# One row-sum addition of 2048 columns instead of two of 1024 in the self attention of a diffusion block

## The reference, cut to what matters

```python
def _attn(xq, ctx, wq, wkv, wo, bo):
    q = _heads(xq @ wq)
    k, v = jnp.split(ctx @ wkv, 2, axis=-1)
    ...
    q = _rope(q, sq, cq)
    k = _rope(k, sk, ck)
    sim = jnp.einsum('bhnd,bhmd->bhnm', q, k) * DH ** (-0.5)
    a = jax.nn.softmax(sim, axis=-1)
    o = jnp.einsum('bhnm,bhmd->bhnd', a, v)
    o = o.transpose(0, 2, 1, 3).reshape(xq.shape[0], xq.shape[1], MID)
    return o @ wo + bo
attn_in = _adaln(x, cond, ln1_w, ln1_b, g1_w, g1_b, b1_w, b1_b)
x = _attn(attn_in, attn_in, sa_wq, sa_wkv, sa_wo, sa_bo) + x
...
```

## Time and profile before

| | |
|---|---|
| time, median of 3 runs | 2244.72 us (2241.64 to 2246.07) |
| the profiled execution's own time | 2244.09 us |
| its span in the profile | 2242.2 us |
| TensorE (PE) busy | 2056.6 us, 92% |
| VectorE (DVE) busy | 1794.6 us, 80% |
| ScalarE (ACT) busy | 1378.4 us, 61% |
| additions at L1098 | 384 + 64, 452.7 + 75.5 us |

### The profile page before, as it was taken

The page is one execution under the profiler, slowest core; times in us unless marked ns, Lnnn a source line. Parts: engine busy times, 40 slices in busy tenths (PEclk is TensorE's granted clock), DMA queues, the critical chain, the costliest instruction groups (busy, mean ns, idle before and its releaser), DMA issues. The chain is left out here.

```text
span 2242.2 us, 40840 instructions
## 1 busy us (share of the span) xinstructions
PE 2056.6 (92%) x16376; PEld 932.5 (42%) x16376; DVE 1794.6 (80%) x2801; ACT 1378.4 (61%) x1748; POOL 35.0 (2%) x26
## 2 busy tenths in 40 slices
PE   4799999999999999999999999997379999986999
PEld 2233333345333335433333533335233444444676
DVE  5888999986899997799999689965768888844654
ACT  4577777765777766677677476762547666633442
POOL 1000000000000000000000000000400000000000
PEclk8799999999999999999999999998589999987999
DMA  5010101111110100111110111003323343324111
GB/s 189 29 39 30 48 30 58 40 39 42 55 39 30 67 37 23 61 45 39 39 39 30 48 59 38 30 20 97 91 81 116 111 124 125 120 73 130 38 39 38
DMA packets 102116, 136.04 MB, mean 61 GB/s; under 512 B 36694, under 2 KB 75176, under 8 KB 101928
## 3 DMA queue, kind: packets, MB, share of 16 engines
q1 hardware_dynamic: 101927, 133.43, 18.2%
HBM read 67.89 MB, written 13.11 MB: 36 GB/s over the span
## 5 line engine op out<-in xcount | busy, mean ns | idle before, releaser
L943 ACT ACTIVATE sa_probs<-sa_ps_s 128x1024 f32<-128x1024 f32 x512 | 496.3, 1021 | 216.1 <-PE sa_ps_s L734 216.1
L749 PE MATMUL sa_ps_o<-sa_probs,sa_v_pair 128*64 128x512 f32 x2048 | 530.9, 610 | 7.4 <-DVE sa_mx L1085 7.4
L1098 DVE TENSOR_TENSOR sa_acc<-sa_acc,sa_probs 128x1024 f32<-128x1024 f32 x384 | 452.7, 1220 | 16.5 <-ACT sa_probs L943 8.2
L1085 DVE CUSTOM_DVE_ANT_0 sa_rise<-sa_ps_t,sa_rise 128x512 f32<-128x512 f32 x504 | 327.1, 686 | 133.9 <-PE sa_ps_t L711 131.1
L931 ACT ACTIVATE sa_rise<-sa_ps_t 128x1024 f32<-128x1024 f32 x252 | 257.4, 1022 | 156.3 <-PE sa_ps_t L704 156.1
L727 PE MATMUL sa_ps_s<-sa_hi 64*128 64x512 f16 x1024 | 197.0, 377 | 0.9 <-ACT sa_raw L917 0.9
L727 PE MATMUL sa_ps_s<-sa_lo,sa_hi 64*128 64x512 f16 x1024 | 197.0, 377 | 0.0
L727 PE MATMUL sa_ps_s<-sa_hi,sa_lo 64*128 64x512 f16 x1024 | 196.8, 377 | 0.0
L749 PEld LDWEIGHTS sa_ps_o<-sa_probs,sa_v_pair 128*64 128x64 f32 x2048 | 114.7, 135 | 164.6 <-issue 96.4
L704 PE MATMUL sa_ps_t<-sa_kd,sa_hi 64*128 64x512 f16 x504 | 99.8, 390 | 33.2 <-ACT sa_raw L917 19.9
L704 PEld LDWEIGHTS sa_ps_t<-sa_kd,sa_hi 64*128 64x128 f16 x504 | 26.1, 93 | 216.6 <-issue 173.5
(11 more groups left out here) (329 smaller groups left out, 4020.7 us busy)
## 6 DMA issues: line engine op xcount, KB each, us to landing
sa_swp<-sa_raw SPq DMA_DIRECT2D x124, 256.0 KB, 2.4
sa_inv<-sa_scratch SPq DMA_DIRECT2D x128, 128.0 KB, 2.9
ca_swp<-ca_raw SPq DMA_DIRECT2D x64, 256.0 KB, 2.4
ca_inv<-ca_scratch SPq DMA_DIRECT2D x64, 256.0 KB, 3.9
sa_xs<-in_x SPq DMA_DIRECT2D x4, 1024.0 KB, 5.8
sa_xr<-in_x SPq DMA_DIRECT2D x4, 1024.0 KB, 5.8
cap_xs<-x_after_self SPq DMA_DIRECT2D x4, 1024.0 KB, 6.9
x_after_cross<-ca_xr SPq DMA_DIRECT2D x32, 128.0 KB, 2.0
```

The lines of the kernel that those rows point to most:

```text
L749: ins = pe.matmul(ps_o[rows(x), half(c)], v_pair[:, kt, rows(x)], probs[:, kt % 2, c, half(x)], start=(kt == 0), stop=(kt == NK - 1))
L943: act.activation(probs[:, kt % 2, c, :], ps_s[c][:, :], ACT.Exp, scale=float(DH) ** -0.5).then_inc(s_p, 1)
L1085: dve.tensor_tensor_reduce(out=larger, in0=max_banks(j, t)[:, half(x)], in1=larger, scale=1.0, scalar=-3.0e38, op0=ALU.add, op1=ALU.max, a ...
L1098: dve.tensor_tensor(acc[:, c, :], before, probs[:, kt % 2, c, :], ALU.add).then_inc(s_acc[c], 1)
```

## The change

The two additions of a slot (c = 0, 1), each 128 x 1024, become one of 128 x 2048 over both halves, which are adjacent in `acc` and in `probs`. It waits until both exponentials of the slot are done (`s_p` at 2 * kt + 2). The two semaphores `s_acc[0]` and `s_acc[1]` become one, which `totals` and the exponentials wait for.

```diff
-        s_acc = [sem("s_acc0"), sem("s_acc1")]
+        s_acc = sem("s_acc")
...
             def totals(g):
-                for c in range(2):
-                    pe.wait_ge(s_acc[c], (NK - 1) * (g + 1))
+                pe.wait_ge(s_acc, (NK - 1) * (g + 1))
...
                     act.wait_ge(s_pv, 2 * NK * gp + 2 * kp + c + 1)
-                    act.wait_ge(s_acc[c], (NK - 1) * gp + max(1, kp))
+                    act.wait_ge(s_acc, (NK - 1) * gp + max(1, kp))
...
-            def add_probs(g, kt, c):
-                dve.wait_ge(s_p, 2 * NK * g + 2 * kt + c + 1)
+            def add_probs(g, kt):
+                dve.wait_ge(s_p, 2 * NK * g + 2 * kt + 2)
                 if kt == 1:
-                    before = probs[:, 0, c, :]
+                    before = probs[:, 0, :, :]
                     if g >= 1:
                         dve.wait_ge(s_sum, g)
                 else:
-                    before = acc[:, c, :]
-                    dve.wait_ge(s_acc[c], (NK - 1) * g + kt - 1)
-                dve.tensor_tensor(acc[:, c, :], before, probs[:, kt % 2, c, :], ALU.add).then_inc(s_acc[c], 1)
+                    before = acc[:, :, :]
+                    dve.wait_ge(s_acc, (NK - 1) * g + kt - 1)
+                dve.tensor_tensor(acc[:, :, :], before, probs[:, kt % 2, :, :], ALU.add).then_inc(s_acc, 1)
...
                     if g >= 0 and kt >= 1:
-                        for c in range(2):
-                            add_probs(g, kt, c)
+                        add_probs(g, kt)
```

## The result

The changed kernel takes 2307.93 us (median of 4 runs, 2302.91 to 2308.62), the kernel before, run beside it, 2245.38 (2241.64 to 2246.07). The ratio is 1.0277 with a 95% interval of 1.0258 to 1.0296: 62.5 us **slower**. That is 9.9 above the forecast of 2298 and inside the range. The profiled execution of the change is its fastest, 2302.91 with a span of 2301.0; against the span of 2242.2 before that is 58.8 more. All that follows is the working of these 58.8.

What follows compares the result with a forecast made beforehand. TensorE was taken to set the pace, VectorE following closely. Plain groups 48.4, normalising groups 4.9 and the end 0.9 summed to 54 us slower, 2298 us, with a range of 2268 to 2322.

Steps and rivals of the forecast that it cites:

- 0.85 later: VectorE work behind the merged addition starts at P + 4.94, not P + 4.09; P starts the slot's bases on TensorE.
- the operation's price: One VectorE addition of 2048 columns takes 2.29 us; work behind it starts after 2.21, saving 0.07 per pair.
- The lateness: VectorE's next maxima beyond P + 0.43: 4.94 + other work - slot length - 0.43; 0.06 to 1.15 us by slot.
- the cover: Lateness of the maxima that TensorE hides by multiplying values: 0.38 us, read from slot 5 of group 8.
- The gap in slot 5: TensorE already idles 0.40 us there waiting for ScalarE's evacuation; the 0.67 stall eats that first, leaving 0.27.
- 1.73 a plain group: TensorE stalls of 0.77, 0.27 and 0.69 us in slots 3, 5 and 7; 48.4 us over 28 groups.
- three long groups 9, 17, 25, which I count as covered: Self-attention groups with slots of twice the length; counted as losing nothing.
- The normalising groups: Groups 2, 3, 10, 11, 18, 19, already past the cover: three slots pay 0.85 each, 2.55 instead of 1.73.
- The clock: Rival: TensorE's pauses drop its granted clock to 1.2 GHz in one group of ten; 2420 us, chance 0.05.
- The cover was no wider: Rival it answers: TensorE has work in hand for 1.15 us, all stalls vanish; 2245 us, chance 0.05.
- Other waits: Rival: waits like the 0.40 in slot 5 take half of the stalls; 2271 us, chance 0.10.
- Faster: Rival: VectorE runs so late it never awaits the second exponential; up to 16 us go, 2228, chance 0.05.

Runs made afterwards that it cites:

- e1: Against the changed kernel: two additions of 1024 columns again, both waiting for the slot's second exponential; 2314.01 us, ratio 1.0306.
- e2: Against the changed kernel: two additions, each waiting for its own exponential, with the change's single counter kept; 2245.03 us, ratio 0.9995.
- e6: Against the changed kernel: merged in slots 2, 4 and 6 only, two additions in slots 1, 3, 5 and 7; 2299.57 us, ratio 1.0243.
- e10: Against the changed kernel: two additions in groups 9, 17 and 25, counter raised by one for every addition; 2299.74 us, ratio 1.0237.
- e11: Against the changed kernel: merged only in slots 4, 5 and 7, behind the other work, not in groups 9, 17, 25; counter by one; 2243.53 us, ratio 0.9991.
- e9: Against the changed kernel: same instructions and order, counter raised by two for each addition and all waits on it doubled; 2313.56 us, ratio 1.0297.
- e4: Against the changed kernel: two additions in groups 9, 17 and 25, merged additions raising the counter by two; 2306.4 us, ratio 1.0264.

## Why the prediction was right, and where it was off

**The wait.** The step "0.85 later" and the operation's price held to the hundredth (2.29, P + 2.73, P + 4.94), and e1 shows that the wait alone makes the loss. e2 shows that the single semaphore costs nothing.

**The lateness and the cover.** All six predicted latenesses are within 0.07 of the rows. Read as the prediction read it, from the first value matmuls to what follows them, the distance is now 721.89 - 720.19 = 1.70 in slot 3, 731.97 - 730.38 = 1.59 in slot 5 and 742.05 - 740.43 = 1.62 in slot 7, where it was 0.91. The pauses are thus 0.79, 0.68 and 0.71, and lateness less pause gives a cover of 0.36, 0.37 and 0.37: the 0.38, read from one slot of another group, held within 0.02. But slots 3 and 7 grew by 0.83 and 0.76, 0.04 and 0.05 more than the pause; in slot 3 the value matmuls behind it take 1.01 up to the next differences, 0.96 before. What is paid is 0.32 less than the lateness there. The gap in slot 5 ate more than its idle time: the differences start 1.43 after the second value matmuls before (707.48 to 708.91) and 0.96 now (733.29 to 734.25), 0.47, where I took 0.40. So the term "1.73 a plain group" measured 1.83, 2.8 us more over 28 groups. That the stalls come from the additions of slots 2, 4 and 6 is shown by e6.

**The term that failed** is "three long groups 9, 17, 25, which I count as covered": put at nothing, they cost 2.45 each, 7.3 in all. It failed in two ways. I looked only at the next maxima and not at the other VectorE work that TensorE waits for. In those groups a residual addition stands behind the slot's addition in slots 1, 2 and 4, and TensorE's next differences wait for it. VectorE before, slot 2 of group 9:

```profile
493.51 0.69 DVE L1085 CUSTOM_DVE_ANT_0 sa_rise<-sa_ps_t,sa_rise 128x512 f32<-128x512 f32 x1 [2.20 <-PE sa_ps_t L711]
...
499.45 0.42 DVE L1120 SCALAR_TENSOR_TENSOR sa_xr<-sa_ps_t,sa_xr 128x256 f32<-128x256 f32 x1
501.96 0.69 DVE L1085 CUSTOM_DVE_ANT_0 sa_rise<-sa_ps_t,sa_rise 128x512 f32<-128x512 f32 x1 [2.09 <-PE sa_ps_t L711]
```

And after:

```profile
509.46 0.69 DVE L1084 CUSTOM_DVE_ANT_0 sa_rise<-sa_ps_t,sa_rise 128x512 f32<-128x512 f32 x1 [2.09 <-PE sa_ps_t L711]
...
516.25 0.42 DVE L1119 SCALAR_TENSOR_TENSOR sa_xr<-sa_ps_t,sa_xr 128x256 f32<-128x256 f32 x1
518.76 0.69 DVE L1084 CUSTOM_DVE_ANT_0 sa_rise<-sa_ps_t,sa_rise 128x512 f32<-128x512 f32 x1 [2.09 <-PE sa_ps_t L711]
```

The residual addition starts 5.94 after the maxima before, 6.79 now; the slot grows from 8.45 to 9.30. Both differences are 0.85, paid whole, because the idle 2.09 between the residual addition and the next maxima is the same: TensorE must have the addition before it can make the bases that VectorE waits for there. Slot 2 pays 0.86 on TensorE in this way, slot 4 0.82 and slot 1 0.20; the 6 new waits of L704 are those of slots 2 and 4.

The second way is slot 7. The "slots of twice the length" are the slots 1 to 6 of these groups (8.05 to 9.85 in group 9, where a plain group has 4.03 to 5.79), and not slot 7: it takes 5.73, like that of a plain group. Its addition is followed by four operations of the output split, and then by the maxima of group 10. VectorE after, and TensorE's bases and the projection that waits:

```profile
559.90 0.42 DVE L1112 CAST sa_o_hi<-sa_o_pair 128x512 f16<-128x512 f32 x1
...
562.03 0.68 DVE L1084 CUSTOM_DVE_ANT_0 sa_rise<-sa_ps_t,sa_rise 128x512 f32<-128x512 f32 x1
```

```profile
560.68 0.39 PE L711 MATMUL sa_ps_t<-sa_hi 64*128 64x512 f16 x2
...
562.77 0.41 PE L350 MATMUL sa_ps_t<-xT_hi,sa_wk_hi 128*64 128x512 f16 x2 [0.36 <-DVE sa_mx L1084]
```

The maxima are 562.03 - 560.68 - 0.43 = 0.92 late (0.06 before), and TensorE pays 0.55. The prediction's own rule would have said so: the four operations take 562.03 - 559.90 = 2.13, so 4.94 + 2.13 - 5.73 - 0.43 = 0.91 late, and 0.91 - 0.38 = 0.53. 0.20 + 0.86 + 0.82 + 0.55 is the 2.45 within rounding. e10, which undoes the change in these groups alone, takes all of it away, 7.3 by the rows and 8.2 by the medians.

**The normalising groups** were to pay 0.85 in three slots, "0.8 extra each = 4.9"; on TensorE they grow by 2.12 each, which is 6 x (2.12 - 1.83) = 1.7 extra. Slots 5 and 0 do pay 0.84 and 0.85; their maxima were 0.80 and 0.73 late before, past the cover. Slot 3 was not past it: 0.31 late before, 1.15 now (group 10), and it pays 0.44. The cover leaves 1.15 - 0.37 = 0.78 of it, and the stall eats a wait, as in slot 5 of the plain groups: the waits of L704 for ScalarE's normalised rows fell from 12 times and 2.4 us to 6 times and 1.2, so by 0.2 in each of the six. The remaining 0.14 I did not trace to a row, and no run tests it.

**The sum.** Against the forecast of 54 the long groups cost 7.3 more, the plain term 2.8 more and the normalising groups 3.2 less: 61. What is left over (groups 8 and 16 together 0.9 more, the first two and the last ones about as much less) cancels. The first group's maxima come 1.2 earlier in the profiled execution of the change, which leaves 59.8, what the last row sums moved by; all behind them was 1.0 shorter, which makes the 58.8 of the span. The medians differ by 62.5, 3.7 more, because the profiled execution of the change is 5.0 below its median and that of before 1.3 below. That the total came this close owes something to luck: 10.1 too little in two terms and 3.2 too much in the third partly cancel.

**The rivals.** The clock stayed at 1.00 in the plain group, and its mean over the span was 0.966 (0.962 before). The cover was no wider than read (0.36 and 0.37). Other waits took 0.47 of a plain group's stalls, not half. "Faster" would need an addition whose turn comes after both exponentials in every slot; e11 makes that so in three slots by placing it last, and there merging costs nothing and gives back a little in the groups past the cover, none in the plain ones. The page Perfetto Trace Analysis of the Trainium skill, section Optimizing Scalar/DVE Operations, says both that grouping helps a saturated engine and that breaking up may finish work sooner where bubbles appear on others; the runs agree with the second sentence for slots 2, 4 and 6 of this kernel (e6: 54 us above the kernel with two additions). The first shows only in groups where VectorE's maxima were already later than the cover, by 0.1 to 0.6 us a group in e11, which the median of the whole kernel doesn't resolve.

**What stays open.** Only the additions' place, number and counting were varied. One exponential of 2048 columns, or an addition that lags its exponentials by a whole slot, was not tried.

## What to carry to other kernels

Merging two operations moves the start of the first to the time when the last input is there. Hold what that delays against the cover of the engine that waits, slot by slot with the length of each slot and not that of the average one. Do so not only for the obvious consumer: go through everything that is queued behind the merged operation and ask for each item who waits for it. Where the engine's turn came after all inputs anyway, merging cost nothing here, and it gave something back only where that engine set the pace.

## What was not expected of the hardware

A merged VectorE addition that raises its semaphore by two, with every wait on it doubled, started 0.089 us after the exponential that it waits for (e9); with one it started 0.032 after. On 28 groups with three waiting slots that is about 0.057 x 3 x 28 = 4.8 us, and the kernels differ by 5.6 (2313.56 to 2307.93) and by 6.7 (e4 to e10).

It is the raise that does it, and not the doubled values. e1 waits for the same doubled values, but each of its additions raises the counter by one, and they start 0.032 after the exponential (729.51 + 1.94 = 731.45 and 731.48 in its rows). In e6 both kinds stand in one kernel: the merged additions, which raise by two, start at 0.089, and the six single ones that waited, which raise by one, at 0.032 to 0.033. Whether other operations, engines or larger steps behave the same was not tried.
